# Middle taps of a depthwise convolution: two of eight blocks added by TensorE as it turns them, in place of one

## What is computed

```
y = einsum('bnh,boh->bno', x, W[subject]) + bias            # conditional linear, 256 -> 256
h = bit_linear(y, w1)                                       # 8-bit tokens, ternary weights, 256 -> 1024
h = depthwise_conv1d(h.transpose(0, 2, 1), conv_w, conv_b)  # 3 taps along the tokens, padding 1
h = jax.nn.silu(h.transpose(0, 2, 1))
x = x + bit_linear(h, w2)                                   # 8-bit tokens, ternary weights, 1024 -> 256
```

## Time and profile before

| what | value |
|---|---|
| time, 3 runs | 293.48, 294.62, 294.82 us, median 294.62 |
| profiled execution: its own time, its span | 293.92 us, 292.0 us |
| busy share of the span | PE 91%, PEld 66%, DVE 87%, ACT 81%, POOL 89% |
| the chain that ended last, by engine | PE 29%, POOL 28%, issue 19%, DVE 8%, ACT 8% |
| TensorE instructions (matmul) | 1762 |
| granted TensorE clock, mean | 0.97 |

### The profile page before, as it was taken

The page is one execution under the profiler, slowest core; times in us unless marked ns, Lnnn a source line. Parts: engine busy times, 40 slices in busy tenths (PEclk is TensorE's granted clock), DMA queues, the critical chain, the costliest instruction groups (busy, mean ns, idle before and its releaser), DMA issues.

```text
span 292.0 us, 6500 instructions
## 1 busy us (share of the span) xinstructions
PE 265.6 (91%) x1762; PEld 192.5 (66%) x1774; DVE 255.2 (87%) x616; ACT 236.2 (81%) x396; POOL 260.2 (89%) x377
## 2 busy tenths in 40 slices
PE   6739999999999999999989989999999999969895
PEld 6516666556665576666667867686877868746794
DVE  0369998888999999868999999999999999999773
ACT  2199999997886884785669979989899898989780
POOL 4359999989899899899999999999999999999871
PEclk9755999999999999999999999999999999999999
DMA  5994788986656754595411525266482633943383
GB/s 156 306 312 125 236 251 249 247 165 177 164 117 158 163 101 108 117 165 126 111 33 37 114 60 129 64 104 148 114 176 77 111 73 72 182 110 92 90 217 110
DMA packets 104870, 41.37 MB, mean 142 GB/s; under 512 B 89157, under 2 KB 102265, under 8 KB 104834
## 3 DMA queue, kind: packets, MB, share of 16 engines
q1 hardware_dynamic: 98384, 32.86, 50.1%
q10 hardware_dynamic: 6450, 8.10, 8.7%
HBM read 16.04 MB, written 4.19 MB: 69 GB/s over the span
## 4 chain that ended last, share of the span: by engine, by line
PE 29%; POOL 28%; issue 19%; DVE 8%; ACT 8%; DMA 4%; SPq 2%; POOLq 0%; ACTq 0%; DVEq 0%
PE banks L1491 6%; POOL raw_all L949 5%; POOL r L885 5%; PE banks L1451 4%; PE banks L1526 3%; PE banks L1549 3%; DMA raw_all<-in_w1a 3%; PE banks L1428 3%; DVE raw_all L1191 2%; POOL mid L939 2%; PE banks L1578 2%; POOL raw_all L813 2%; DVE apad L1179 2%; POOL xs L854 2%; DVE am L1197 1%
## 5 line engine op out<-in xcount | busy, mean ns | idle before, releaser
L949 POOL TENSOR_TENSOR raw_all<-raw_all,mid 128x1024 f32<-128x1024 f32 (+1 forms) x31 | 55.3, 1785 | 0.0
L686 ACT ACTIVATE banks<-apad,taps 128x512 f32<-128x512 f32 x64 | 44.4, 700 | 6.2 <-DVE apad L1179 6.0
L1191 DVE SCALAR_TENSOR_TENSOR raw_all<-apad,taps,banks 128x512 f32<-128x512 f32 x64 | 46.8, 740 | 0.7 <-ACT banks L686 0.2
L1179 DVE SCALAR_TENSOR_TENSOR apad<-banks,low_up,dqb 128x512 f32<-128x512 f32 x64 | 46.4, 743 | 0.3 <-PE banks L1526 0.2
L1128 DVE TENSOR_REDUCE am<-g 128x1 f32<-128x1024 f32 x32 | 38.8, 1212 | 5.1 <-ACT g L639 5.0
L939 POOL TENSOR_SCALAR mid<-apad,taps,convb 128x512 f32<-128x512 f32 x56 | 42.4, 763 | 0.0
L639 ACT ACTIVATE g<-banks,dqz 128x1024 f32<-128x1024 f32 x32 | 35.5, 1110 | 8.0 <-PE banks L1432 4.4
L1197 DVE TENSOR_REDUCE am<-g 128x1 f32<-128x1024 f32 x30 | 36.2, 1207 | 2.1 <-ACT g L697 2.1
L885 POOL TENSOR_SCALAR r<-g,qs 128x1024 uint16<-128x1024 f32 x32 | 35.8, 1119 | 2.3 <-DVE qs L1140 1.8
L1526 PE MATMUL banks<-ryT,tern 128*128 128x512 f16 x128 | 35.9, 379 | 2.1 <-DVE raw_all L1191 1.9
L697 ACT ACTIVATE g<-banks 128x1024 f32<-128x1024 f32 x30 | 30.7, 1024 | 6.3 <-PE banks L1555 5.0
(11 more groups left out here) (162 smaller groups left out, 615.5 us busy)
## 6 DMA issues: line engine op xcount, KB each, us to landing
xs<-in_x ACTq DMA_DIRECT2D x7, 512.0 KB, 3.6
out_y<-xs SPq DMA_DIRECT2D x14, 256.0 KB, 2.5
x2T<-in_xT ACTq DMA_DIRECT2D x4, 512.0 KB, 3.6
wl<-in_cwl SPq DMA_DIRECT2D x8, 256.0 KB, 3.0
xT<-in_xT ACTq DMA_DIRECT2D x3, 512.0 KB, 6.2
cw<-in_cw SPq DMA_DIRECT2D x16, 64.0 KB, 4.3
raw_all<-in_w1a SPq DMA_DIRECT2D x1, 1024.0 KB, 7.7
raw_all<-in_w2a SPq DMA_DIRECT2D x1, 1024.0 KB, 6.2
```

The costliest lines, as they stand in the source:

```text
L686: act.activation(bank(BANK_U[g % 3]), apad[:, f, 2:S + 2], ACT.Copy, scale=taps[:, f, 2:3]).then_inc(p_last, 1)
L949: pool.tensor_tensor(c[:, 2 * q:2 * q + n, :], c[:, 2 * q:2 * q + n, :], mid[q % 2][:, 0:n, :], ALU.add).then_inc(p_sum, 1)
L1179: dve.scalar_tensor_tensor(out=apad[:, f, 1:S + 1], in0=bank(BANK_U[(KH * b + f) % 3]), scalar=low_up[:, f:f + 1], in1=dqb[b % 2][:, :], o ...
L1191: dve.scalar_tensor_tensor(out=conv[b % 2][:, f, :], in0=apad[:, f, 0:S], scalar=taps[:, f, 0:1], in1=bank(BANK_U[(KH * b + f) % 3]), op0= ...
```

## The change

TensorE takes the middle taps of blocks 6 and 7 in every batch, as it did in batch 7 alone. `tap_sum(b, 3)` is gone in batches 0 to 6. `mid_last` holds two blocks per batch parity. GpSimd sums three pairs a batch, and the two buffers of `mid` go on alternating over the batches: pair q of batch b uses buffer (3b + q) mod 2. The middle tap of block 6 now waits, as that of block 7, for the last turning of the batch two before; `transpose_conv(b, 0)` waits for three sums a batch.

```
-        mid_last = [sb(f"mid_last{k}", [P, S]) for k in range(2)]
-        def turned(b):
-            return KH - 2 if b == B - 1 else KH - 1
+        mid_last = [sb(f"mid_last{k}", [P, 2, S]) for k in range(2)]
+        KS = KH - 2
         def middle(b, f):
-            return mid[f // 2 % 2][:, f % 2, :] if f < KH - 1 else mid_last[b % 2][:, :]
+            return mid[((TB - 1) * b + f // 2) % 2][:, f % 2, :] if f < KS else mid_last[b % 2][:, f - KS, :]
...
-                if f < KH - 1:
-                    wait(pool, p_sum, TB * b + f // 2 - 1)
+                if f < KS:
+                    wait(pool, p_sum, (TB - 1) * b + f // 2 - 1)
                 else:
                     wait(pool, p_cT[TB - 1], b - 1)
...
             def tap_sum(b, q):
-                if 2 * q >= turned(b):
-                    return
                 c = conv[b % 2]
-                n = min(2, turned(b) - 2 * q)
-                pool.wait_ge(p_first, KH * b + 2 * q + n)
-                pool.wait_ge(p_mid, KH * b + 2 * q + n)
-                pool.tensor_tensor(c[:, 2 * q:2 * q + n, :], c[:, 2 * q:2 * q + n, :],
-                                   mid[q % 2][:, 0:n, :], ALU.add).then_inc(p_sum, 1)
+                pool.wait_ge(p_first, KH * b + 2 * q + 2)
+                pool.wait_ge(p_mid, KH * b + 2 * q + 2)
+                pool.tensor_tensor(c[:, 2 * q:2 * q + 2, :], c[:, 2 * q:2 * q + 2, :], mid[((TB - 1) * b + q) % 2][:, :, :],
+                                   ALU.add).then_inc(p_sum, 1)
...
                 on(tap_sum, s - 1, 2)
                 on(middle_tap, s - 1, 7)
-                on(tap_sum, s - 1, 3)
...
-                    pe.wait_ge(p_sum, TB * b + (turned(b) + 1) // 2)
+                    pe.wait_ge(p_sum, (TB - 1) * (b + 1))
...
-                for f in range(turned(b)):
+                for f in range(KS):
...
-                for f in range(turned(b), KH):
+                for f in range(KS, KH):
```

More of the change, by code:

```diff
@@ L1021, in first @@
                 middle_tap(0, 5); middle_tap(0, 6); tap_sum(0, 2); scale_of_down1(7, 1); round1(7, 2)
-                middle_tap(0, 7); tap_sum(0, 3); residual(6, 1); residual(7, 0); middle_tap(1, 0); round1(7, 3)
+                middle_tap(0, 7); residual(6, 1); residual(7, 0); middle_tap(1, 0); round1(7, 3)
                 spread_of_up(2); middle_tap(1, 1); middle_tap(1, 2); add_down1(6); middle_tap(1, 3); tap_sum(1, 0)
                 tap_sum(1, 1); middle_tap(1, 4); scale_of_down(0, 0); middle_tap(1, 5); middle_tap(1, 6)
-                tap_sum(1, 2); tap_sum(1, 3); middle_tap(1, 7); round2(0, 2); middle_tap(2, 0); residual(7, 1)
+                tap_sum(1, 2); middle_tap(1, 7); round2(0, 2); middle_tap(2, 0); residual(7, 1)
                 middle_tap(2, 1); scale_of_down(0, 1); middle_tap(2, 2); tap_sum(2, 0); middle_tap(2, 3)
```

## The result

The changed kernel took 295.98 us (median of 16 runs, 294.31 to 297.43) against 294.60 us for the kernel before (16 runs): ratio 1.0053, 95% interval 1.0033 to 1.0073. The predicted median was 295.8 us, 0.4% slower.

What follows compares the result with a forecast made beforehand. The prediction took a loop of TensorE and ScalarE to bound the slots; 0.22 before slot 3, 1.32 in the slots and -0.33 at the end gave +1.2 us, a median of 295.8 us, range 293.6 to 297.6.

Steps and rivals of the forecast that it cites:

- GpSimd does not bound the slots: In the slots nobody waits for GpSimd's backlog, so removing 7.56 us of its sums was costed at nothing there.
- the loop: Slots 3 to 6: 11.5 us of TensorE and 6.4 us of ScalarE, repeating every 17.96 us, set the slot.
- 0.11 us a matmul: Each matmul added to a turned tile costs TensorE 0.11 us; 28 cost 3.1 us if all were on the path.
- Three turnings of a slot in the loop, 0.33 us: Slots 3 to 6: turnings (s-2, 3), (s-1, 0), (s-1, 1) each pay one matmul; 1.32 us over four slots.
- Ahead of slot 3, 0.22 us: Before slot 3, two of five turnings shift turning (1, 3) by 0.22 us, with 0 and 0.55 as ends.
- Slot 7, nothing: In slot 7 VectorE bounds with unchanged work and the turnings have time, so nothing is added to its 15.50 us.
- The end, -0.33 us: At the end silu(7, 0) stops waiting for GpSimd, waits for turning (7, 0), and gains 0.33 us.
- The new wait for `mid_last`: In front of middle_tap(s, 6), waiting for turning (s-2, 3), it costs nothing as GpSimd reaches block 6 late.
- The sum: Whole kernel: +1.2 us on the profiled execution's 293.92 us; predicted median 295.8 us, 0.4% slower.
- VectorE's idle time a slot: In the slots it grows from 0.26 to about 0.6 us, in front of `first_tap` and `absmax_y`.

Runs made afterwards that it cites:

- e2: The kernel before with one more matmul in each turned tile of batches 0 to 6, GpSimd's work left as it was; 295.57 us, ratio 1.0052.
- e3: The changed kernel without the added matmul in batches 0 to 6, so block 6's middle tap is made but not added; 293.93 us, ratio 0.9984.
- e5: The changed kernel with the added matmul left out in tile 3 of batches 0 to 6; 296.09 us, ratio 1.0058 to the kernel before.
- e6: The changed kernel with the added matmul left out in tiles 0 and 1 of batches 0 to 6; 294.41 us, ratio 1.0006 to the kernel before.
- e4: The kernel before, with TensorE adding block 6's middle tap in batch 6 too, and in no other; 294.10 us, ratio 0.9988.
- the third profile: The changed kernel profiled a third time, no edit; one run, 297.36 us.
- e1: The changed kernel again, no edit, for a second profile; 295.93 us, ratio 1.0060 to the kernel before.
- e7: The kernel before with TensorE's register load of linear moved from behind up(s, 2) to behind up(s-1, 7) in the slots; 294.12 us, ratio 0.9995.
- e9: The kernel before with e7's register-load move, and TensorE adding block 6 in batch 6 too; 293.15 us, ratio 0.9962.
- e10: The kernel before with e7's register-load move, and TensorE adding block 6 in batches 0 and 6 too; ratio 0.9990.
- e8: The changed kernel with the same register-load move as e7; 294.54 us, ratio 1.0006 to the kernel before.

## Why the prediction was right, and where it was off

- **GpSimd does not bound the slots, TensorE's time on the loop does: right.** Shown by e2 and e3, each of which does one half of the change alone. But the loop is not "closed by TensorE and ScalarE alone", as the prediction has it. From `linear` at 222.03 to the last result of turning (4, 1), 230.46, it is 8.4 us of TensorE; from there ScalarE works without idle time not only to silu(4, 2) but on to last_tap(5, 7), 7.8 us; then come first_tap(5, 7) on VectorE, 0.8 us, and up(6, 2) with the register load, 0.9 us, up to the next `linear`: 17.96 us together. Turnings (s-2, 3) and (s-2, 2) lie beside that path.
- **0.11 us a matmul: right**, 1.09 us a tile.
- **Three turnings of a slot in the loop, 0.33 us: off.** It was two, 0.22 us (e5, e6), so four slots cost 0.91 us and not 1.32. The step that failed is the reading that `linear`'s start at 222.03 follows turning (s-2, 3) through `lead`. It follows a register load behind up(s, 2), which waits for VectorE's first_tap(s-1, 7), and turning (s-2, 3) ended ahead of that. The rows that show it are those of the weight loads.
- **Ahead of slot 3, 0.22 us: measured 0.26.** Of it, tiles 0 and 1 make about 0.16 (e6 has 29.06 us there).
- **Slot 7, nothing: measured 0.09 to 0.15.** e4 has 0.09 too with batch 6's turnings alone, and so has e6 with tiles 2 and 3 alone, which points at turning (6, 2), ahead of down2(5, 2). That it runs from there through `dequant2` to ScalarE is argued only.
- **The end, -0.33 us: measured -0.26 and -0.33 in two profiles, +0.03 in the third.** As foreseen, silu(7, 0) now waits for TensorE (0.99 us in the first profile) and not for GpSimd. The reason was half of it: e3 shows that fewer sums give the 0.34, and e2 that longer slots give 0.18 of it without them. Why the third profile has none of it (turning (7, 0) starts 3.58 us behind (6, 3) there, 3.29 and 3.22 in the other two) is not shown.
- **The new wait for `mid_last`: nothing, as said.**
- **The sum.** By the stretches up to silu(7, 0), the change costs 0.26 + 0.91 + 0.09 - 0.33 = 0.93 us in e1's profile and 1.01 in the first, 0.3%. The timed ratios, 0.53% (0.33 to 0.73) and 0.60% (0.40 to 0.81), are 1.4 and 1.9 us by the medians, so 0.4 to 0.9 us of the timed loss have no place in the stretches. (The lower end of the first interval is 1.0 us and reaches down to their sum, that of the second is 1.2 and does not.) The 0.6 to 1.0 us behind silu(7, 0) would fill the gap, but e2 and e5 have the ratio and not the wait, so I don't count them in; the gap stays open. That the median came within 0.2 us of the 295.8 predicted is therefore in part luck: the slots were put 0.41 us too high, and something outside the sum made up for it.
- **VectorE's idle time a slot**, foreseen at 0.6 us, is 18.18 - 17.80 = 0.38, as the slot grew by less.

## What to carry to other kernels

An engine that is busy for 100% of a stretch need not bound it: look for who waits for it, and test it by taking work off it (e3: 1.7 us less a slot, no change). In a loop over several engines, cost an added instruction by what stands between it and the next hand-over: a wait for another engine on the way swallows what lies ahead of it, as the wait for `first_tap` did here with and without the pause behind it, while a fixed pause behind such a wait is on the path (e7). And an engine with a backlog can become the bound once the loop is shortened (e7). A relief brought something there when it lay behind the engine's last idle time, and next to nothing ahead of a wait (e9 against e10).

## What the runs showed of the hardware

A `value_load` between two matmuls kept TensorE's weight loads 0.8 us apart (221.22 to 222.01, 222.42 to 223.22), with 0.63 and 0.53 us of idle time; with the `value_load` moved away the same two stood 0.25 us apart in e7 and 0.40 in e8 (221.58 and 221.43 to 221.83). Moving it made four slots 1.23 us shorter. Turning by matmul ran at a distance of 0.11 us at a granted clock of 1.00, with some 40 of a slot's 125 matmuls being such.
